# Layer 1's last three rows of blocks: one more quarter of E turned by DMA in rows 29 and 30, and the work around them reordered

## The reference

```python
deg = jnp.clip(adj.sum(axis=1), 1.0); dis = deg ** (-0.5)
adj_norm = dis[:, None] * adj * dis[None, :]
sim = x @ x.T / (norms[:, None] * norms[None, :])
attn = softmax(beta * sim * adj, axis=1)
l0 = adj_norm @ x - x + sigmoid(alpha) * (attn @ x - x)
x = layernorm(x + l0)
x = layernorm(x + relu(adj @ (x @ weights)))
```

## Time and profile before

| | us |
|---|---|
| median of 3 runs | 654.17 |
| lowest and highest run | 653.23, 655.1 |
| the profiled execution | 653.43 |
| its span | 651.6 |
| TensorE busy | 637.5 |
| VectorE busy | 516.1 |
| ScalarE busy | 413.7 |
| POOL busy | 236.9 |

### The profile page before, as it was taken

One profiled execution on the slowest core, in us unless ns is written; L12 is line 12 of the kernel. 1 busy time (PEld: TensorE's weight loads), 2 busy tenths in 40 slices (PEclk: granted clock), 3 DMA queues, 4 the chain that ended last, 5 costly groups with the idle time before them and its releaser, 6 DMA issues.

```text
span 651.6 us, 16130 instructions
## 1 busy us (share of the span) xinstructions
PE 637.5 (98%) x5095; PEld 464.9 (71%) x5095; DVE 516.1 (79%) x1564; ACT 413.7 (63%) x774; POOL 236.9 (36%) x249
## 2 busy tenths in 40 slices
PE   8889999999999999999999999999999999999996
PEld 7457777777777777777777777888888864444465
DVE  5989999999999999999999998868777763334453
ACT  7999999999999999999999998712211110000000
POOL 5999544544544544544644646400000000000000
PEclk9999999999999999999999999999999999999999
DMA  7879999999999999999999996500000000000001
GB/s 280 315 158 260 295 236 247 294 248 246 298 244 246 299 243 241 296 251 248 303 234 254 293 249 105 101 2 2 0 0 0 0 1 1 16 17 18 16 32 33
DMA packets 167100, 107.89 MB, mean 166 GB/s; under 512 B 146464, under 2 KB 150688, under 8 KB 167072
## 3 DMA queue, kind: packets, MB, share of 16 engines
q1 hardware_dynamic: 167072, 107.57, 62.7%
HBM read 69.27 MB, written 2.10 MB: 110 GB/s over the span
## 4 chain that ended last, share of the span: by engine, by line
PE 90%; DVE 3%; ACT 2%; DMA 2%; issue 1%; POOL 1%; SPq 0%; DVEq 0%; ACTq 0%; POOLq 0%
PE ps_s L1023 23%; PE ps_s L1227 17%; PE ps_e L1199 15%; PE ps_acc L1060 8%; PE ps_e L1034 8%; PE ps_e L1060 8%; PE ps_acc L1063 4%; PE ps_e L1063 4%; DMA x_keep<-in_x 1%; DMA eTx<-e_parts 1%; DVE scores L723 1%; ACT scores L537 1%; PE ps_s L1076 1%; PE ps_acc L1211 1%; PE ps_at L1076 1%
## 5 line engine op out<-in xcount | busy, mean ns | idle before, releaser
L1023 PE MATMUL ps_s<-xn_parts,xn_signed 128*128 128x512 f16 x756 | 203.3, 379 | 2.9 <-DVE cmax L723 2.9
L723 DVE CUSTOM_DVE_ANT_1 scores<-ps_s,adj_bytes 128x512 f32<-128x512 f32 x252 | 171.6, 683 | 21.4 <-PE ps_s L1023 14.6
L537 ACT ACTIVATE scores<-scores,col 128x1024 f32<-128x1024 f32 x128 | 157.4, 1232 | 1.2 <-DVE col L734 0.9
L496 ACT ACTIVATE adj_bytes<-land 128x1024 uint8<-128x1024 f32 x128 | 133.5, 1047 | 0.6 <-POOL packed L354 0.6
L362 POOL TENSOR_SCALAR e_parts<-scores 128x1024 f16<-128x1024 f32 x64 | 68.5, 1070 | 153.3 <-ACT scores L537 149.9
L1199 PE MATMUL ps_e<-y_parts,stage 128*128 128x256 f16 x896 | 98.0, 273 | 0.0
L1023 PEld LDWEIGHTS ps_s<-xn_parts,xn_signed 128*128 128x128 f16 x756 | 68.6, 98 | 38.4 <-DVE cmax L723 2.5
L1199 PEld LDWEIGHTS ps_e<-y_parts,stage 128*128 128x128 fp8e4 x896 | 87.7, 98 | 10.1
L544 ACT ACTIVATE eT_parts<-ps_e 128x512 f16<-128x512 f32 x126 | 74.8, 595 | 24.4 <-PE ps_e L1034 23.4
L744 DVE SCALAR_TENSOR_TENSOR e_parts<-scores,e_parts 128x1024 f16<-128x1024 f32 x64 | 88.2, 1380 | 0.4 <-POOL e_parts L362 0.4
L738 DVE SCALAR_TENSOR_TENSOR eT_parts<-ps_e,eT_parts 128x512 f16<-128x512 f32 x126 | 86.0, 683 | 1.8 <-ACT eT_parts L544 1.8
(11 more groups left out here) (139 smaller groups left out, 974.2 us busy)
## 6 DMA issues: line engine op xcount, KB each, us to landing
land<-in_adj SPq DMA_DIRECT2D x128, 512.0 KB, 5.6
x_keep<-in_x SPq DMA_DIRECT2D x4, 512.0 KB, 5.3
out<-u SPq DMA_DIRECT2D x7, 256.0 KB, 2.1
eTx<-e_parts SPq DMA_TRANSPOSE x64, 4.3
packT<-packed SPq DMA_TRANSPOSE x16, 6.7
out<-u SPq DMA_DIRECT2D x2, 128.0 KB, 1.7
scores<-in_L_gnn_weights SPq DMA_DIRECT2D x1, 64.0 KB, 2.7
col<-in_L_gnn_beta SPq DMA_DIRECT2D x1, 0.5 KB, 7.2
```

The costliest lines, as they stand in the source:

```text
L496: nc.scalar.activation(adj_bytes[:, q, i * CH:(i + 1) * CH], land[:, q, i, :], ACT.Copy, scale=float(BYTE_TOP[q] >> i), accum_out=deg[:, i ...
L537: nc.scalar.activation(piece, piece, ACT.Exp, bias=neg_max[q], scale=abs_beta, accum_out=csum[:, q, i:i + 1]).then_inc(exp_done, 1)
L723: nc.vector.tensor_tensor_reduce(scores[:, q, o:o + BANK].rearrange("p (k q) -> p k q", k=K), score_bank(h, r == 0 if start else False).re ...
L1023: ins = nc.tensor.matmul(score_bank(h, start), xn_signed[:, q, part, :], xn_parts[:, other, o:o + BANK], start=(part == 0 and other == 0), ...
```

## The change

In rows 29 and 30 as well, the second quarter of E goes by way of POOL, VectorE and a DMA turn, and TensorE turns two banks per row in each of the last three rows. There is one buffer for the halves before the turn (`third`) and there are three behind it (`thirdT`), so POOL's high for row 30 and that for row 31 wait for the turn before theirs (`third_turned`). Row 28 leaves the loop and is written out. Row 30's attends 6 and 7 move behind the first sums, and the sums among row 31's attends are reordered. The diff, cut where names and loops only follow:

```diff
@@ -68,8 +68,10 @@
     SLOT = (0, 2, 1, 3)
     FIRST_EXP = (0, 2, 3, 1)
     LAST_EXP = (0, 2, 3, 1)
+    SIX_ATTEND = (0, 4, 1, 5, 6, 7, 2, 3)
+    LATE_ATTEND = (0, 1, 4, 5, 6, 7, 2, 3)
     LAST_ATTEND = (0, 1, 4, 5, 6, 7, 2, 3)
-    LATE_ATTEND = (0, 4, 5, 1, 2, 6, 7, 3)
+    SIX = 29
     W = CH // 4
     assert D == P and C == 4 and H == 8 and R == 32 and Q == 8

@@ -227,7 +229,7 @@
         words = [adj_bytes[:, q, :].bitcast(U32).rearrange("p (i w) -> p i w", i=C) for q in range(2)]
         spare = land[:, 0, :, :].rearrange("p i j -> p (i j)").bitcast(F16)
         third = spare[:, 0:2 * CH].rearrange("p (a j) -> p a j", a=2)
-        thirdT = spare[:, 2 * CH:4 * CH].rearrange("p (t i) -> p t i", i=P)
+        thirdT = [spare[:, (1 + m) * 2 * CH:(2 + m) * 2 * CH].rearrange("p (t i) -> p t i", i=P) for m in range(3)]
...
@@ -290,16 +292,22 @@
             with sp.Fori(2, Q) as b:
                 for k in range(G):
                     turn(b, k)
+            def turn_third(m):
+
+                sp.wait_ge(third_lo, m + 1)
+                sp.dma_start_transpose(thirdT[m], third.rearrange("p a j -> p (a j)")).wait_op(
+                    x_loaded[0], 16, "sem-ge").then_inc(third_turned, 16)
+
             turn_ex(R - 3, 1, 1)
+            turn_third(0)
             turn_ex(R - 2, 0, 0)
             turn_ex(R - 2, 0, 1)
             turn_adj(R // 2 - 1, 1)
+            turn_third(1)
             turn_ex(R - 1, 1, 0)
             turn_ex(R - 1, 1, 1)
-            sp.wait_ge(third_lo, 1)
-            sp.dma_start_transpose(thirdT, third.rearrange("p a j -> p (a j)")).wait_op(
-                x_loaded[0], 16, "sem-ge").then_inc(third_turned, 16)
-            sp.wait_ge(e_turned, R * TB - 2)
+            turn_third(2)
+            sp.wait_ge(e_turned, R * TB - 6)
             sp.wait_ge(ex_lo, 2 * R)
             sp.dma_start(wts, weights).then_inc(w_loaded, 16)
             with sp.Fori(0, Q - 1) as g:
@@ -361,6 +369,16 @@
                     pool.wait_ge(ex_turned[n], r * 16)
                 nc.gpsimd.tensor_scalar(e_parts[:, n, 0, :], scores[:, q, (n + 2) * CH:(n + 3) * CH], E_SCALE, 1.0,
                                         ALU.mult, ALU.mult).wait_op(sign_done, 1, "sem-ge").then_inc(ex_hi, 1)
+
+            def third_high(m):
+
+                pool.wait_ge(exp_done, (SIX + m) * C + C)
+                if m == 0:
+                    pool.wait_ge(cast_done, (R - 1) * C)
+                else:
+                    pool.wait_ge(third_turned, 16 * m)
+                nc.gpsimd.tensor_scalar(third[:, 0, :], scores[:, (SIX + m) % 2, CH:2 * CH], E_SCALE, 1.0,
+                                        ALU.mult, ALU.mult).wait_op(sign_done, 1, "sem-ge").then_inc(third_hi, 1)

...
             pack(R - 2, 0, R // 2 - 1, 1)
+            third_high(0)
...
             ex_high(R - 2, 0, 0)
             ex_high(R - 2, 0, 1)
+            third_high(1)
             pack(R - 1, 1, R // 2 - 1, 1)

             pool.wait_ge(dis_done, 1)
@@ -458,10 +478,7 @@
             y_rows(2)
             ex_high(R - 1, 1, 0, place=1)
             ex_high(R - 1, 1, 1, place=1)
-            pool.wait_ge(exp_done, R * C)
-            pool.wait_ge(cast_done, R * C)
-            nc.gpsimd.tensor_scalar(third[:, 0, :], scores[:, 1, CH:2 * CH], E_SCALE, 1.0,
-                                    ALU.mult, ALU.mult).wait_op(sign_done, 1, "sem-ge").then_inc(third_hi, 1)
+            third_high(2)
...
@@ -575,29 +592,41 @@
...
                 row(r, 0)
                 row(r + 1, 1)
+            row(R - 4, 0)
+
+            def late_e_high(m, b, order):
+                act.wait_ge(e_turned, SIX * TB + (2 * m + b + 1))
+                act.wait_ge(attn_part, (SIX - 1 + m) * H + (order.index(b) + 1))
+                nc.scalar.activation(eT_parts[:, b, 0, :], ps_e[:, b, :], ACT.Copy, scale=E_SCALE).then_inc(e_hi, 1)
+
+            for h in range(H):
+                if h in (0, 2):
+                    late_e_high(0, h // 2, ATTEND_ORDER)
+                if h < C:
+                    cast(R - 1, 1, h)
+                else:
+                    exps(R - 2, 0, EXP_ORDER[h - C])

...
-            e_high(R - 2, 0)
-            e_high(R - 2, 1)
+            late_e_high(1, 0, SIX_ATTEND)
+            late_e_high(1, 1, SIX_ATTEND)
             act.wait_ge(deg_done, 1)
             nc.scalar.activation(dis[:, :], dis[:, :], ACT.Sqrt).then_inc(deg_root, 1)
             nc.scalar.activation(table_loads[1], eps_c, ACT.Exp)
-            e_high(R - 2, 2)
             exps(R - 1, 1, 0, LAST_EXP)
             y_high(0)
-            e_high(R - 2, 3)
+            late_e_high(2, 0, LATE_ATTEND)
+            late_e_high(2, 1, LATE_ATTEND)
             exps(R - 1, 1, 2, LAST_EXP)
+            y_high(1)
             exps(R - 1, 1, 3, LAST_EXP)
-            e_high(R - 1, 0, order=LATE_ATTEND)
-            e_high(R - 1, 1, order=LATE_ATTEND)
-            y_high(1)
             exps(R - 1, 1, 1, LAST_EXP)
             y_high(2)
...
@@ -865,34 +896,62 @@
                 row(r, 0)
                 row(r + 1, 1)
...
-            for n in range(C * (G - 1)):
+            for n in range(C * (G - 1) - 1):
                 row(R - 14 + n, n % 2, spread=(n // C, n % C))

+            def late_e_low(m, b):
+                dve.wait_ge(e_hi, SIX * TB + (2 * m + b + 1))
+                nc.vector.scalar_tensor_tensor(eT_parts[:, b, 1, :], ps_e[:, b, :], E_SCALE,
+                                               eT_parts[:, b, 0, :], ALU.mult, ALU.subtract).then_inc(e_lo, 1)
+
+            def third_low(m):
+
+                dve.wait_ge(third_hi, m + 1)
+                nc.vector.scalar_tensor_tensor(third[:, 1, :], scores[:, (SIX + m) % 2, CH:2 * CH], E_SCALE,
+                                               third[:, 0, :], ALU.mult, ALU.subtract).then_inc(third_lo, 1)
+
+            mask(R - 2, 0, 4)
+            late_e_low(0, 0)
+            mask(R - 2, 0, 5)
+            ex_low(SIX, 1, 1)
+            mask(R - 2, 0, 6)
+            late_e_low(0, 1)
+            mask(R - 2, 0, 7)
+            row_max(R - 2, 0)
+            stage_block(G - 2, G - 2, (C - 1,))
+            total_step(SIX, 1, 0)
+            mask(R - 1, 1, 0)
+            third_low(0)
+            total_step(SIX, 1, 1)
+            mask(R - 1, 1, 1)
+            ex_low(R - 2, 0, 0)
+            attn_add(R - 4, 0)
+            mask(R - 1, 1, 2, third_row=True)
+            total_step(SIX, 1, 2)
+            mask(R - 1, 1, 3, third_row=True)
+
             mask(R - 1, 1, 4)
-            e_low(R - 2, 0)
+            late_e_low(1, 0)
             ex_low(R - 2, 0, 1)
             mask(R - 1, 1, 5)
+            late_e_low(1, 1)
             mask(R - 1, 1, 6)
             degrees()
             mask(R - 1, 1, 7)
             row_max(R - 1, 1)
-            e_low(R - 2, 1)
+            third_low(1)
             total_step(R - 2, 0, 0)
             total_step(R - 2, 0, 1)
-            e_low(R - 2, 2)
-            y_low(0)
-            e_low(R - 2, 3)
             attn_add(R - 3, 1)
             total_step(R - 2, 0, 2)
-            e_low(R - 1, 0)
-            e_low(R - 1, 1)
+            y_low(0)
+            late_e_low(2, 0)
+            late_e_low(2, 1)
             y_low(1)
             ex_low(R - 1, 1, 0)
             ex_low(R - 1, 1, 1)
             y_low(2)
-            dve.wait_ge(third_hi, 1)
-            nc.vector.scalar_tensor_tensor(third[:, 1, :], scores[:, 1, CH:2 * CH], E_SCALE, third[:, 0, :],
-                                           ALU.mult, ALU.subtract).then_inc(third_lo, 1)
+            third_low(2)
             attn_add(R - 2, 0)
             y_low(3)
             for n in range(3):
...
-            with pe.Fori(2, R - 3, 2) as r:
+            with pe.Fori(2, R - 5, 2) as r:
                 row(r, 0)
                 row(r + 1, 1)
-
-            turn_e(R - 2, 0, 0)
-            cosines(R - 1, 1, 4)
-            turn_e(R - 2, 0, 1)
-            cosines(R - 1, 1, 5)
-            attend(R - 3, 1, 5)
-            cosines(R - 1, 1, 6)
-            attend(R - 3, 1, 6)
-            attend(R - 3, 1, 7)
-            cosines(R - 1, 1, 7)
+            row(R - 4, 0)
+
+            def late_turn_e(m, b, order=EXP_ORDER):
+                if b == 0:
+                    pe.wait_ge(exp_done, (SIX + m) * C + (order.index(0) + 1))
+                pe.wait_ge(e_lo, SIX * TB + (2 * m + b - 1))
+                for n in range(TH):
+                    t = TH * b + n
+                    ins = nc.tensor.transpose(ps_e[:, b, n * P:(n + 1) * P], scores[:, (SIX + m) % 2, t * P:(t + 1) * P],
+                                              ident[:, :])
+                ins.then_inc(e_turned, 1)
+
+            def six_attend(k):
+                attend(SIX, 1, k, order=SIX_ATTEND, six=0)

             def late_attend(k):
-                attend(R - 2, 0, k, order=LATE_ATTEND)
-
-            late_attend(0)
-            turn_e(R - 2, 0, 2)
-            late_attend(1)
-            late_attend(2)
-            late_attend(3)
```

(47 more changed lines are left out.)

20 lines of the change are left out of this document (12 added, 8 removed).

## The result

The changed kernel takes 656.66 us (median of 6 runs, 655.45 to 656.96), the kernel before 654.23 (6 runs, 653.23 to 655.10): ratio 1.0032, 95% interval 1.0022 to 1.0043, 2.4 us more. Its profiled execution took 656.78 us with a span of 654.9.

The account below looks back on a forecast made before the run. TensorE was taken as the bound, with little VectorE slack. Y low 2's end at 419.8 plus 12.7 us put the output rows at 432.5, 2.0 us later; added to the profiled 653.43 this gave 655.4 us, range 652.4 to 656.8.

Parts of the forecast that it names:

- the stretch: From row 29's first turn to the first output row; the output rows were forecast to start 2.0 us later.
- the race for Y low 0: In the kernel before, VectorE's Y low 0 just beats POOL's product 2 to the port; losing would cost 1.7 us.
- The border: Slower than the kernel before by over 0.3% (1.96 us, above 656.13 us): chance 0.22; within 0.3%: 0.68.
- Third high 0 at 388.3: POOL's new high for row 29 makes VectorE's low issued at 388.31 wait, taking 1.8 us; VectorE 0.6 us late.
- Row 30's low moved up: Low of row 30's first DMA half after mask 1 delays mask 2 and cosines 4, losing 0.88 us plus 0.5 to 1.4.
- the tie with the next high: Row 30's moved low waits perhaps 0.9 us more if POOL's next high gets the port first.
- Third turn and POOL: POOL's high 1 waits for row 29's third turn (4.7 us landing), pack and Y products behind it; POOL 1.5 us late.
- Y lows: VectorE's Y lows collide with POOL's products and highs; Y low 2 ends at 419.75, two microseconds later than before.
- Waits: Sign of being right: TensorE waits over 1 us for Y low 0 and again for Y low 2.
- The port costs nothing: Rival, 12%: POOL and VectorE collisions cost nothing on this path; output rows 1.4 us earlier, 652.0 us.
- No new wait: Rival, 5%: 1.76 us of turns and both idle times saved, 2.9 us; 650.5 us.
- The third turn's landing as a clear loss: Rival, 18%: the turn POOL waits for lands after 5.6 us, Y low 2 0.9 us later still; 656.3 us.

Follow-up runs that it names:

- a_peel_front: Changed kernel with row 2 written out ahead of the loops instead of row 28 behind them: median 656.24 us against 655.10, ratio 1.0014 to the kernel before.
- a_exlow_back: Changed kernel with the low of row 30's first DMA half back behind mask 3 of row 31: 655.92 us against 655.16, ratio 1.0024 to the kernel before.
- a_own_buffer: Changed kernel with a separate buffer for row 30's third half, so POOL's high needn't await row 29's turn: 655.84 us against 655.16, ratio 1.0011 to the kernel before.
- port_alone: Separate kernel running only POOL and VectorE operations of this kernel's shapes in pairs: a low behind a high ends 2.13 us after the high's start.
- b_unrolled: Kernel before with rows 28 and 29 written out of the TensorE and ScalarE loops, same work and order: 655.89 us against 655.10, ratio 1.0011.
- c_y2_sooner: Changed kernel, third highs on ScalarE with own buffer, row 30's low back, Y low 2 earlier, last attends later: 654.37 us against 654.50, ratio 1.0005 to kernel before.

## Why the prediction was right, and where it was not

Times of the changed profile are given less 1.45 us here, so that they stand on the scale of the prediction.

- **The time.** Forecast 655.4 and a range to 656.8; measured 656.66, near its upper end, and 656.16 in the repeat. Forecast 2.0 us more in the stretch; measured 1.82, and 1.45 where the clock stayed up. The first comparison's 2.4 us hold more than the stretch, and the profile started 1.45 us later; the repeat measured 1.7. So the size of the change was right, and the point was low for another reason. The 2.0 us were added to the profiled execution (653.43), one of the fastest of the kernel before, and not to the median (654.17), which gives 656.2. The reason given, that the median run loses part of the race for Y low 0, no profile of the kernel before shows: Y low 0 won in both.
- **The border.** The ratio, 1.0032, lies just over the 0.3% to which the forecast gave only 0.22; the repeat, 1.0027, lies within it.
- **Third high 0 at 388.3.** Wrong in place. The low issued at 385.28 took 1.75, since it waited behind the pack's add instead of going ahead of it as before. That moved VectorE past the high, and the low at 388.77 took 1.22. VectorE was half a microsecond late all the same. That it came out so is luck: in a_peel_front the low behind the high took 1.77, as foretold.
- **Row 30's low moved up.** The mechanism was right, the size too large: it waited 0.27 us for POOL's high, and the tie with the next high never came, since that one waited for a landing until 395.70. So mask 2 started at 396.98 (forecast 397.4 to 398.4), cosines 4 at 397.73 (forecast 398.2 to 399.1). a_exlow_back prices it at 0.7.
- **Third turn and POOL.** Right: high 1 at 399.03 (399.35), Y products at 404.10 (404.6). The POOL chain I counted 1.5 us late was 1.0 late. a_own_buffer shows why removing the wait alone gives only half of it: the degrees are nearly as late.
- **Y lows.** Y low 0 took 1.67 behind product 1 and ended at 409.91 (410.4), the first sums started at 410.06 (410.5). Y low 2 ended at 419.04 (419.75): this term was 0.7 too large. Behind it I had TensorE start at once; the slow clock, of which I had no term, gave 0.5 back. Two errors of opposite sign make the sum look better than it is.
- **Waits.** Over 1 us for Y low 0: 2.18. Again for Y low 2: not in this profile, where the slow clock filled it; 1.01 in a_peel_front.
- **The rivals.** The port costs nothing: refuted by port_alone. No new wait: refuted. The third turn's landing as a clear loss: row 29's third, for which POOL waits, landed after 4.5 us, not 5.6. The time lies near that rival's 656.3 for another reason, the base of the sum.
- **The race for Y low 0 in the kernel before.** Foretold as 1.7 us; b_unrolled shows it lost: Y low 0 took 1.6 us more, and TensorE waited 1.91. In two batches, of 29 and 35 runs, the kernel before had 11 and 7 runs over 656.3 us, in the others none of 34. That these are lost races is not shown, for none of them was profiled.
- **Not foreseen: the cut loops.** I treated "row 28 leaves the loop" as free. Over 657 us lie 19 of 89 runs of kernels with rows 28 and 29 written out at the end, 2 of 36 with row 2 in front, 1 of 98 of the kernel before. b_unrolled shows that this belongs to the written out code; 2 of 36 against 19 of 89 may still be chance in part. The path is not settled. The larger instruction fetches in the DMA rows fall at 376 to 379 and 391 to 394 us in the former, at 401 in the kernel before (the expectation of b_unrolled had put that at 394, where only small ones are); with row 2 in front the first of the two is gone and the second is not. The second comes too late to start the delay of row 29's first turn (b_unrolled, above); whether the first does, through what stands on the queue, wasn't tested.

  The Trainium skill (Runtime: NRT & Kernel Launch, Instruction fetch mechanics) calls fetches mostly hidden and says that kernels prefer full unrolling. The rows here do not bear the second out at the end of this loop: b_unrolled, with two more rows written out, ran from 653.94 to 657.62 us and gained nothing over the kernel before.

## What to carry to other kernels

When the work taken from the bound engine is handed to two engines that share a port, price the collisions first: two 1 us operations that meet cost the second almost all of the first. Then look at which chain the bound engine waits for at the next join. Here Y low 0 ended 23.0 us after row 29's first turn before, and 23.8 or later in every variant that takes all four banks from TensorE, so the 1.76 us of work taken away turned into waiting. Y low 2 came 1.7 us sooner in c_y2_sooner, and then the next join waited. And rewriting a loop's end is an edit of its own: time it alone.

## What the hardware showed that I had not expected

- VectorE operations as small as 8 columns, with one SBUF input, wait for a whole POOL operation (1.05 us instead of 0.17, 1.89 behind a Y product).
- The clock fell after some idle times of 2.2 us and stayed up after others of 2.1 to 2.6: in the changed kernel 4.28 us for 24 matmuls instead of 2.62. Where the clock stayed up (a_peel_front) a wait of 1.01 us followed, so most of the loss was hidden: the stretch was 0.37 us longer.
- The same DMA turn landed after 4.2 and 4.3 us in the kernel before, and after 7.1 to 7.4 in three profiles of kernels with the same turn and other code, each time with the turn before it on the queue under way for 3.1 us or more when it was issued.
